# Expert rows rounded up to 64 instead of 128: 60 full blocks and 8 blocks of two halves

## The reference, cut to what matters

```python
logits = h @ gate_W + gate_b
top1 = argmax(logits)
for e in range(8):
    mask = (top1 == e)
    g = gelu(h * mask @ W1[e] + b1[e])        # 128 -> 512
    out = out + (g @ W2[e] + b2[e]) * mask    # 512 -> 128
x = x + gb * out
```

## Time and profile before

| | us |
|---|---|
| median of 3 runs | 363.47 |
| lowest, highest | 361.49, 364.53 |
| span of the profiled execution | 360.6 |
| TensorE busy in it | 338.8 (94%) |
| VectorE busy | 271.2 (75%) |
| ScalarE busy | 265.1 (74%) |
| GpSimd busy | 213.2 (59%) |

### The profile page before, as it was taken

The page is one execution under the profiler, slowest core; times in us unless marked ns, Lnnn a source line. Parts: engine busy times, 40 slices in busy tenths (PEclk is TensorE's granted clock), DMA queues, the critical chain, the costliest instruction groups (busy, mean ns, idle before and its releaser), DMA issues.

```text
span 360.6 us, 13729 instructions
## 1 busy us (share of the span) xinstructions
PE 338.8 (94%) x4823; PEld 263.9 (73%) x4823; DVE 271.2 (75%) x1104; ACT 265.1 (74%) x644; POOL 213.2 (59%) x262
## 2 busy tenths in 40 slices
PE   6899999899988999998999999999999999999994
PEld 5445765566465566646665669999989999999993
DVE  3456997898879789878887978887677676666653
ACT  2688988799878888977888756676656667666761
POOL 3142386776667757857854618846767455545554
PEclk9999999999999999999999999999999999999999
DMA  7174656774566547444432467445657665545410
GB/s 233 50 253 166 210 184 221 259 243 160 177 227 205 176 167 230 163 132 156 153 133 100 149 163 227 142 118 150 194 161 269 209 184 147 147 128 135 137 38 12
DMA packets 40211, 60.47 MB, mean 168 GB/s; under 512 B 5426, under 2 KB 28086, under 8 KB 40016
## 3 DMA queue, kind: packets, MB, share of 16 engines
q1 hardware_dynamic: 33776, 42.54, 39.9%
q0 software_dynamic: 6368, 17.05, 12.5%
HBM read 28.63 MB, written 19.34 MB: 133 GB/s over the span
## 4 chain that ended last, share of the span: by engine, by line
PE 60%; ACT 15%; DMA 10%; DVE 6%; issue 5%; POOL 1%; SPq 1%; DVEq 1%; POOLq 0%; ACTq 0%
PE ps_proj L1350 16%; PE ps_feat L1337 9%; DMA qmix<-qsqs 9%; PE ps_proj L1132 6%; PE ps_den_gate L1337 4%; PE ps_proj L1182 4%; PE ps_kv L1337 4%; ACT qf L627 3%; ACT qvals L606 2%; ACT shared L588 2%; PE ps_kv L1198 2%; PE ps_out L1330 2%; ACT den L656 2%; ACT shared L581 2%; ACT kvm L600 2%
## 5 line engine op out<-in xcount | busy, mean ns | idle before, releaser
L545 POOL DMA_INDIRECT out<-kf,modb x71 | 70.1, 987 | 52.4 <-DVE kf L1060 47.0
L507 POOL DMA_INDIRECT experts_lists<-pay,slot x64 | 65.9, 1030 | 43.4 <-DVE slot L893 29.5
L1350 PE MATMUL ps_proj<-w2sb,qf 128*128 x568 | 75.0, 275 | 0.4 <-ACT qf L690 0.4
L1350 PEld LDWEIGHTS ps_proj<-w2sb,qf 128*128 128x128 f32 x568 | 68.9, 192 | 0.6 <-issue 0.6
L681 ACT ACTIVATE xT<-ps_out 128x128 f32<-128x128 f32 x71 | 19.7, 277 | 44.8 <-PE ps_out L1330 44.1
L1055 DVE TENSOR_TENSOR kf<-ps_proj,firsts_sb 128x128 f32<-128x128 f32 x71 | 20.7, 291 | 34.6 <-PE ps_proj L1350 22.6
L690 ACT ACTIVATE qf<-ps_feat,shared 128x128 f32<-128x128 f32 x144 | 40.9, 374 | 0.0
L1337 PE MATMUL ps_feat<-xT,shared 128*128 128x128 f32 x288 | 38.8, 277 | 1.5 <-issue 0.9
L1337 PEld LDWEIGHTS ps_feat<-xT,shared 128*128 128x128 f32 x288 | 35.0, 192 | 2.8 <-issue 1.7
L1132 PE MATMUL ps_proj<-shared,wsb 128*128 128x512 f32 x62 | 33.3, 620 | 1.0 <-ACT shared L581 0.4
L977 DVE COPY shared<-firsts_sb 128x516 f32 x71 | 31.4, 442 | 1.6 <-issue 1.5
(11 more groups left out here) (189 smaller groups left out, 890.3 us busy)
## 6 DMA issues: line engine op xcount, KB each, us to landing
modb<-experts_lists SPq DMA_DIRECT2D x71, 196.0 KB, 2.8
xall<-in_x SPq DMA_DIRECT2D x16, 256.0 KB, 3.0
pay<-modb SPq DMA_DIRECT2D x16, 256.0 KB, 3.0
qmix<-qvals SPq DMA_DIRECT2D x30, 128.0 KB
qmix<-qsqs SPq DMA_DIRECT2D x30, 128.0 KB
modb<-modulation_rows SPq DMA_DIRECT2D x4, 768.0 KB, 5.2
firsts_sb<-in_firsts SPq DMA_DIRECT2D x8, 322.0 KB, 4.2
w2sb<-in_w SPq DMA_DIRECT2D x8, 256.0 KB
```

What stands on the lines that cost most here:

```text
L507: g_.indirect_dma_start(out=lists, in_=pay[b.home][:, t, :], in_offset=None, out_offset=bass.IndirectOffsetOnAxis(ap=slot[b.home][:, t:t + ...
L545: g_.indirect_dma_start(out=rows_out, in_=yb[u], in_offset=None, out_offset=bass.IndirectOffsetOnAxis(ap=token, axis=0), bounds_check=last ...
L1350: ins = mm(Y[u % 2][:, 0:D], g[u % R4][:, c * P:(c + 1) * P], w2sb[:, bass.ds(e * DFF + c * D, D)], start=(c == 0), stop=(c == FC - 1))
```

## The change

The lists are rounded up to 64 rows instead of 128. 60 full blocks (`NFULL`) hold pairs of 64 rows; what is left of each expert after its full blocks, at most 16 halves (`NHALF`), goes into 8 split blocks, each of two halves of 64 rows with an expert each. That makes 68 blocks. The split ones are k = 46, 49, 52 and so on to 67, the last.

A split block has two loads of 64 rows (SyncE); two copies of first weights, now in 6 buffers, and one copy of the second half's second weights to `w2c` (VectorE); `hidden` with four matmuls for each half, 64 moving rows each; eight gelu instructions of 64 columns; `second` with four matmuls for each half, 64 stationary columns each, to partitions 0 to 63 and 64 to 127 of the result; and two adds of the second bias. The tables get a third part for the halves: block_counts(1) has three more steps, the update of `done` is now also done for part 1, `half_counts` is new, `block_ends`, `block_columns` and `table_rows` run once more, at k = 33 to 38, and TensorE turns two more columns at k = 37. SyncE and TensorE wait for the third table before the first split block.

```diff
 FC = DFF // P
-NBLK = NT + E - 1
+HALF = P // 2
+NFULL = (NT * 2 - E) // 2
+NHALF = 2 * E
+NBLK = NFULL + NHALF // 2
 U = 12
 R4 = 4
+RF = 6
 EARLY_ROWS = 4
...
 PADS_FROM = EARLY - E - 4
+LATE = NFULL - EARLY
+SPLIT_FROM = NBLK - 3 * (NHALF // 2)
 PITCH = NT * P + P
...
+class Block:
+    def __init__(self, k):
+        self.k, self.u = k, k % U
+        self.split = k >= SPLIT_FROM and (k - SPLIT_FROM) % 3 == 2
+        splits = max(0, k - SPLIT_FROM) // 3
+        self.turn = splits
+        full = k - splits
+        self.entries = [NFULL + 2 * splits, NFULL + 2 * splits + 1] if self.split else [full]
+        self.copies = range(k + splits, k + splits + len(self.entries))
+BLOCKS = [Block(k) for k in range(NBLK)]
+BLOCK_OF_COPY = [block.k for block in BLOCKS for _ in block.copies]
+FIRST_SPLIT = next(block.k for block in BLOCKS if block.split)
+def loads_of(k):
+    return sum(len(block.entries) for block in BLOCKS[k % U:k + 1:U])
 class Steps:
...
-        shared = sb("shared", [P, max(R4 * WB2, 4 * L)])
+        shared = sb("shared", [P, max(RF * WB2, 4 * L)])
         xn1_, hT, kvals, ksqs = (shared[:, n * L:(n + 1) * L] for n in range(4))
...
         nblk = sb("nblk", [P, E])
+        halves = sb("halves", [P, E])
         endblk = sb("endblk", [P, E])
...
         tmp = sb("tmp", [P, 2, E])
-        blk_e = sb("blk_e", [P, NBLK], I32)
-        blk_row = sb("blk_row", [P, NBLK], I32)
+        blk_e = sb("blk_e", [P, NFULL + NHALF], I32)
+        blk_row = sb("blk_row", [P, NFULL + NHALF], I32)
...
         xT = [sb(f"xT{u}", [P, P]) for u in range(2)]
-        firsts_c = [shared[:, u * WB2:(u + 1) * WB2] for u in range(R4)]
+        firsts_c = [shared[:, u * WB2:(u + 1) * WB2] for u in range(RF)]
         g = [qf[:, u, :] for u in range(R4)]
+        w2c = [qmix[:, n, :] for n in range(2)]
         kf_row = kf[:, :, :, :, :].rearrange("p c t j k -> p (c t j k)")
...
                     sp.wait_ge(s_yout[u], 16 * (k // U))
-                row = sp.value_load(blk_row[0:1, bass.ds(k, 1)], min_val=0, max_val=PADROW)
-                sp.dma_start(xin[u], lists[bass.ds(row, P), :]).then_inc(s_xin[u], 16)
+                if k == FIRST_SPLIT:
+                    sp.wait_ge(s_blk, 3)
+                n = P // len(BLOCKS[k].entries)
+                for part, entry in enumerate(BLOCKS[k].entries):
+                    row = sp.value_load(blk_row[0:1, bass.ds(entry, 1)], min_val=0, max_val=PADROW)
+                    sp.dma_start(xin[u][part * n:(part + 1) * n, :], lists[bass.ds(row, n), :]).then_inc(s_xin[u], 16)
...
                 act.wait_ge(s_hid, k + 1)
-                for c in range(FC):
-                    ins = a.activation(g[k % R4][:, c * P:(c + 1) * P], HID[k % R4][:, c * P:(c + 1) * P],
-                                       ACT.Gelu, bias=firsts_c[k % R4][:, WB1 + c:WB1 + c + 1])
+                n = P // len(BLOCKS[k].entries)
+                for part, copy in enumerate(BLOCKS[k].copies):
+                    for c in range(FC):
+                        at = slice(c * P + part * n, c * P + (part + 1) * n)
+                        ins = a.activation(g[k % R4][:, at], HID[k % R4][:, at],
+                                           ACT.Gelu, bias=firsts_c[copy % RF][:, WB1 + c:WB1 + c + 1])
                 ins.then_inc(s_gelu, 1)
...
                     v.tensor_copy(cnt_i[:], counts[1]).then_inc(s_cnti, 1)
-                    s.mark(v.tensor_scalar(nblk[:], counts[1], float(P - 1), None, ALU.add))
+                    s.mark(v.tensor_scalar(nblk[:], counts[1], float(HALF - 1), None, ALU.add))
                     s.wait()
                     s.mark(v.tensor_copy(cnt_b[:], nblk[:]))
-                s.wait()
-                s.mark(v.tensor_scalar(cnt_b[:], cnt_b[:], P.bit_length() - 1, None, ALU.arith_shift_right))
+                    s.wait()
+                    s.mark(v.tensor_scalar(cnt_b[:], cnt_b[:], HALF.bit_length() - 1, None, ALU.arith_shift_right))
+                    s.wait()
+                    s.mark(v.tensor_copy(halves[:], cnt_b[:]))
+                s.wait()
+                shift = P.bit_length() - HALF.bit_length() if part else P.bit_length() - 1
+                s.mark(v.tensor_scalar(cnt_b[:], cnt_b[:], shift, None, ALU.arith_shift_right))
                 s.wait()
...
-            def block_ends():
+            def half_counts():
+                s = Steps(dve, s_end, steps[0])
+                s.wait()
+                s.mark(v.tensor_scalar(done[:], done[:], 2.0, None, ALU.mult))
+                s.wait()
+                s.mark(v.tensor_tensor(nblk[:], halves[:], done[:, 0:E], ALU.subtract))
+                steps[0] += s.n
+            def block_ends(rows=P):
...
                 s.wait()
-                s.mark(v.tensor_scalar(jump[:], jump[:], float(PITCH // P), None, ALU.add))
+                s.mark(v.tensor_scalar(jump[:], jump[:], float(PITCH // rows), None, ALU.add))
                 steps[0] += s.n
...
             def block_columns(part):
...
                 s.wait()
-                v.tensor_scalar(tab[:, 1:2], tab[:, 1:2], float(P), float(PADROW), ALU.mult, ALU.min)\
+                v.tensor_scalar(tab[:, 1:2], tab[:, 1:2], float(HALF if part == 2 else P), float(PADROW), ALU.mult, ALU.min)\
                     .then_inc(s_tab, 1)
-                if part == 0:
-                    s.mark(v.tensor_scalar(endblk[:], endblk[:], float(EARLY), None, ALU.min))
-                    dve.wait_ge(s_tab, 1)
+                if part < 2:
+                    s.mark(v.tensor_scalar(endblk[:], endblk[:], float(LATE if part else EARLY), None, ALU.min))
+                    dve.wait_ge(s_tab, part + 1)
                     s.wait()
-                    v.tensor_copy(done[:, 0:1], endblk[:, 0:1])
-                    s.mark(v.tensor_tensor(done[:, 1:E], endblk[:, 1:E], endblk[:, 0:E - 1], ALU.subtract))
+                    v.tensor_tensor(done[:, 0:E], done[:, 0:E], endblk[:], ALU.add).then_inc(s_done, 1)
+                    dve.wait_ge(s_done, part + 1)
+                    s.mark(v.tensor_tensor(done[:, 1:E], done[:, 1:E], endblk[:, 0:E - 1], ALU.subtract))
                     s.wait()
...
             def table_rows(part):
...
-                at, n = (0, EARLY) if part == 0 else (EARLY, NBLK - EARLY)
+                at, n = ((0, EARLY), (EARLY, LATE), (NFULL, NHALF))[part]
                 dve.wait_ge(s_tabT, part + 1)
...
             def expert_of(k):
-                return dve.value_load(blk_e[0:1, bass.ds(k, 1)], min_val=0, max_val=E - 1)
+                return [dve.value_load(blk_e[0:1, bass.ds(entry, 1)], min_val=0, max_val=E - 1)
+                        for entry in BLOCKS[k].entries]
...
             def copy_firsts(k):
...
-                if k >= R4:
-                    dve.wait_ge(s_gelu, k - (R4 - 1))
-                v.tensor_copy(firsts_c[k % R4], firsts_sb[:, bass.ds(expert[k] * WB, WB2)]).then_inc(s_fc, 1)
+                for copy, e in zip(BLOCKS[k].copies, expert[k]):
+                    if copy >= RF:
+                        dve.wait_ge(s_gelu, BLOCK_OF_COPY[copy - RF] + 1)
+                    v.tensor_copy(firsts_c[copy % RF], firsts_sb[:, bass.ds(e * WB, WB2)]).then_inc(s_fc, 1)
+                if BLOCKS[k].split:
+                    if BLOCKS[k].turn >= 2:
+                        dve.wait_ge(s_y, k - 5)
+                    v.tensor_copy(w2c[BLOCKS[k].turn % 2], w2sb[:, bass.ds(expert[k][1] * DFF, DFF)]).then_inc(s_w2c, 1)
                 if k + 1 < NBLK:
...
             def result(k):
...
                 u = k % U
-                y, e = yb[u], expert.pop(k)
+                y, chosen = yb[u], expert.pop(k)
                 dve.wait_ge(s_y, k + 1)
...
                     dve.wait_ge(s_yout[u], 16 * (k // U))
-                v.tensor_tensor(y, Y[k % 2][:, 0:D], firsts_sb[:, bass.ds(e * WB + WB2, D)], ALU.add)\
-                    .then_inc(s_yst, 1)
+                n = P // len(chosen)
+                for part, e in enumerate(chosen):
+                    rows_ = slice(part * n, (part + 1) * n)
+                    ins = v.tensor_tensor(y[rows_, :], Y[k % 2][rows_, 0:D], firsts_sb[rows_, bass.ds(e * WB + WB2, D)],
+                                          ALU.add)
+                ins.then_inc(s_yst, 1)
                 dve.wait_ge(s_yst, 2 * k + 1)
...
                     table_rows(1)
+                if k == 33:
+                    half_counts()
+                if k == 34:
+                    block_ends(HALF)
+                if k == 35:
+                    block_columns(2)
+                if k == 38:
+                    table_rows(2)
             for k in range(NBLK - 2, NBLK):
...
             def transpose_block(k):
-                pe.wait_ge(s_xin[k % U], 16 * (k // U) + 16)
+                pe.wait_ge(s_xin[k % U], 16 * loads_of(k))
                 tr(XT[:, 0:P], xin[k % U][:, H2:H2 + D], ident).then_inc(s_bt, 1)
...
             def hidden(k):
                 u = k
-                pe.wait_ge(s_fc, k + 1)
```

(25 more changed lines are left out.)

4 lines of the change are left out of this document (3 added, 1 removed).

## The result

| | before | after |
|---|---|---|
| median, us | 364.0 (361.49 to 365.58, 4 runs) | 370.5 (368.59 to 371.49, 4 runs) |
| ratio, 95% interval | | 1.0188 (1.0151 to 1.0226) |
| span of the profiled run | 360.6 | 368.1 |
| start of the first block transpose | 211.37 | 212.88 |
| from there to the end of the span | 149.25 | 155.23 |

What follows compares the result with a forecast made beforehand. TensorE was taken to bound the expert stage, 1.90 us per full block. Blocks +3.8, third table +0.44 and +1.4, part 0 +0.1 and end +0.9 gave +6.6 on 363.47: 370.1 us, range 365.0 to 375.5.

Steps and rivals of the forecast that it cites:

- The blocks: Expert stage on TensorE: eight split blocks of 3.09 us replace eleven full ones of 1.90, +3.8 us.
- The third table: Around k = 25 to 38: two more transposes +0.44 us on TensorE, and +1.4 reaching it from VectorE's added steps.
- the 1.25 for the columns: Third table on VectorE: block_columns(2) priced at 1.25 us from the earlier table's step, within a sum of 3.9.
- The end: After the last, split block: eight gelu instructions +0.6 us and a second add of the result +0.3, together +0.9.
- The sum: Whole kernel: 3.8 + 0.44 + 1.4 + 0.1 + 0.9 = +6.6 us, giving 370.1 us, 1.8% slower.
- What is hidden: Split blocks: ScalarE, VectorE, loads and stores cost nothing; VectorE's group of three blocks 6.6 us against TensorE's 6.9.
- the 1.8 for a split block: VectorE's extra work per split block: weight copies, a register load and an add, about 1.8 us.
- VectorE as the bound: Rival: table steps wholly exposed and split blocks costing VectorE 2.4 us, so +11.5, 375 us; chance 0.12.
- The cover of the loads: SyncE's first split load waits for the third table, ready around k = 38, used seven blocks later; cost nothing.
- Columns: Rival: streamed columns price the hidden step, a split block takes 2.22 us, time 363.2 or 361.8; chance 0.08.
- Cheap changes: Rival: array changes in split second steps cost nothing and VectorE's table steps are hidden, +2.6, 366.1 us; chance 0.17.
- No side by side: Rival: halves of split second steps run one after the other, 1.76 us each step, 7.0 more, 377 us; chance 0.08.

Runs made afterwards that it cites:

- wide half: Changed kernel, with half of a split block's hidden instructions streaming 128 columns instead of 64, same result; 369.81 us, ratio 1.0223 to before.
- all second steps in halves: Kernel before, with the second step of all 71 blocks issued for two halves of 64 rows in turn; 381.84 us (one run).
- the last run: Version with 64 full and 4 split blocks, third table and `done` update later, split blocks one place earlier; 361.86 us, ratio 0.9978 to before.
- spread table: Changed kernel, with the third table's steps at k = 35 to 42 instead of 33 to 38; 373.51 us, ratio 1.027 to before.
- the two more copies: Changed kernel, with two added 128x512 copies on VectorE ahead of each split block's copy of second weights; 369.85 us, ratio 1.0219 to before.
- all hidden steps in halves: Kernel before, with the hidden step of all 71 blocks issued in two halves of 64 columns, same weights; 421.54 us (one run).
- both runs on the second step: Changed kernel with one expert's second weights for all rows of split blocks, 366.99 us; kernel before with every second step in halves, 381.84 us.

## Why the prediction was right, point by point

*The blocks* (+3.8 forecast, 3.3 measured). Right in each part: hidden 0.84 instead of 0.87 over a full one, second 0.32 instead of 0.33, a saving of 5.7 for three blocks. The row that carried the hidden step was the start of the kernel with 16 columns: a price measured where the suspected limit stands alone. Only the last of the eight second steps does not pay the 0.32: from its start to the first add behind it is 1.24 us (361.93 to 363.17), against 1.29 in the kernel before. The wide half shows directly that columns cost nothing in the hidden step. For the changes of the array the Trainium skill, page "TensorEngine Tiling (Array Packing)", section "Key Properties", says that a change of tiling mode drains the engine; the run with all second steps in halves shows 0.32 us for two.

*The third table* (0.44 + 1.4 forecast, 2.0 measured). That the sum fits is in part luck; its parts were off in ways that made up for each other. VectorE's added steps take 3.0 us instead of 3.9, counted to the start of the next operation (three more counts 0.42, the update 0.37, half counts 0.32, ends 0.60, columns 0.90, rows 0.38): the 1.25 for the columns held 0.32 in which VectorE stood idle ahead of the copy (277.55 to 277.87), and the new steps do not meet this again each time. More of them reached TensorE than forecast: 2.5 us with the transposes, of which the lost stall of the kernel before gave 0.5 back. And the 0.44 for two transposes was not their own: 0.21 is, as the last run shows. Most of the rest was already a wait for a copy of weights: it ends at 278.30, and the hidden step behind the transposes starts at 278.35.

*The end* (+0.9 forecast, 0.7 measured). The gelu wait grew by 0.56, as forecast by 0.6, and the two adds take 0.59 instead of 0.29, as forecast; from the start of the last store to the end of the span it is 0.15 less (3.42 against 3.57).

*The sum.* The two profiled runs differ by 5.98 in the stage and 0.13 in part 0, 6.1 against the 6.6 forecast; that the medians differ by 6.5 owes something to scatter.

*What is hidden.* Right that VectorE and the loads stay covered, but VectorE's group was mis-sized: 6.06 us, not 6.6. The term that failed is the 1.8 for a split block, which measures about 1.25. The turn with the second register read and the second add takes 2.54 us instead of 1.61, 0.93 more, as forecast. The turn with the two more copies takes 1.94, so these cost 0.33, not 0.84: three copies in a row start some 0.37 us apart, and the register read runs behind them. The chance of 0.12 for VectorE as the bound was rather high on this account. The cover of the loads was called seven blocks and costed at nothing, which held; in the profiled run of the spread table three blocks did not suffice.

*The rivals.* Columns: fell with the wide half and with all hidden steps in halves; a fixed price per instruction, which the prediction did not name, falls with L1215. Cheap changes: fell with both runs on the second step. No side by side: fell. VectorE as the bound: fell in the split blocks; around the tables VectorE did hold up TensorE, as the forecast itself had it.

## What to carry to other kernels

Before rows are packed more tightly into smaller blocks, price the instruction by what limits it: for these float32 matmuls, with a full weight tile and up to 128 moving columns, the load does, and a half block costs a whole one. Weigh surcharge times number, and the work of the new bookkeeping, against the blocks saved: eight surcharges of 1.16 us lost against three blocks of 1.90; four alone would not have, but with the third table where it stood they still lost 0.7%, and with it moved the time was that of the kernel before. Work added to an engine that is not the bound is free only where it has spare turns; count them there, and look at which queue stands behind the new result.

## What the runs showed that was not expected

With the halves issued in turn of four matmuls each, TensorE started the second half's first instruction 0.49 us into the step, ahead of three instructions of the first half that stand before it in the program. The Trainium skill, page "TensorE: Matmul & The Clock Gate", section "The mechanism", has matmuls start strictly in program order; on this row, with two column groups, they do not. Why it started at that instruction and not earlier is open.

When the loads came late in the profiled run of the spread table, the loss was larger than the wait of 2.4 us: TensorE's granted clock fell to a mean of 0.68 and 0.75 over 12 us behind it, and two spacings were 4.47 and 4.80 us.
